# Causal heads in another order, with a bank for their projections and one for sums and values, and compact weights for the folds

## The reference

```python
x = x + tanh(g_xattn[0]) * L0_xattn(layernorm(x), ctx)      # 16 heads of 64, no mask
x = x + tanh(g_ffn[0]) * L0_ffn(layernorm(x))               # ternary weights, 8-bit activations
x = x + tanh(g_xattn[1]) * L1_xattn(layernorm(x), ctx)
x = x + tanh(g_ffn[1]) * L1_ffn(layernorm(x))               # one gated expert, gelu

def L1_xattn(xx, ee):
    x = ln(xx); x = x + mha_a1(x, x, causal)    # 16 heads of 32 over 512 tokens
    x = ln(x);  return x + mha_a2(x, ee)        # 16 heads of 32 over 77 tokens

def mha(x, y, causal):
    q, k, v = ln(x) @ wq, ln(y) @ wk, ln(y) @ wv
    a = softmax(q @ k.T / sqrt(D))              # the softmax runs over all 512 keys
    if causal: a = a * (key > query)            # the mask comes after it
    x = x + concat(a @ v) @ li1 + li1_b
    return x + gelu(ln(x) @ li2 + li2_b) @ li3 + li3_b
```

## Time and profile before

| | us |
|---|---|
| median of 3 runs | 419.72 (417.35 to 419.81) |
| the profiled execution | 419.06 |
| its span | 417.2 |
| PE, PEld busy | 346.0 (83%), 237.8 (57%) |
| DVE, ACT, POOL busy | 307.4 (74%), 279.2 (67%), 114.6 (27%) |

### The profile page before, as it was taken

The page is one execution under the profiler, slowest core; times in us unless marked ns, Lnnn a source line. Parts: engine busy times, 40 slices in busy tenths (PEclk is TensorE's granted clock), DMA queues, the critical chain, the costliest instruction groups (busy, mean ns, idle before and its releaser), DMA issues.

```text
span 417.2 us, 6788 instructions
## 1 busy us (share of the span) xinstructions
PE 346.0 (83%) x2038; PEld 237.8 (57%) x2038; DVE 307.4 (74%) x718; ACT 279.2 (67%) x965; POOL 114.6 (27%) x215
## 2 busy tenths in 40 slices
PE   4978999636377779999798898988997899977796
PEld 4756888513233445555554545567775678853656
DVE  3656678679874798999999899865776787845515
ACT  4465998758134887898888888825626889854061
POOL 5312875200110222232232223323001354420000
PEclk9999999986558999999999999989999899998999
DMA  7920000000003836832951690000000000000001
GB/s 215 348 110 2 2 2 2 0 1 2 0 20 94 198 94 147 183 76 68 206 132 37 149 207 15 2 2 1 2 2 0 0 3 0 2 0 2 1 0 52
DMA packets 8861, 24.75 MB, mean 59 GB/s; under 512 B 2668, under 2 KB 2745, under 8 KB 8569
## 3 DMA queue, kind: packets, MB, share of 16 engines
q1 hardware_dynamic: 8824, 24.32, 23.0%
HBM read 7.00 MB, written 0.52 MB: 18 GB/s over the span
## 4 chain that ended last, share of the span: by engine, by line
PE 41%; DVE 15%; ACT 8%; issue 7%; SPq 2%; POOL 1%; DMA 0%; DVEq 0%; ACTq 0%
PE ps L400 8%; PE ps L540 5%; PE ps L524 5%; DVE nm L1532 4%; PE ps L670 4%; PE ps L618 3%; ACT pring L1145 3%; PE ps L633 3%; PE ps L493 3%; PE ps L473 3%; PE ps L704 2%; PE ps L441 2%; ACT arena L1022 2%; PE ps L686 2%; DVE xn L1216 2%
## 5 line engine op out<-in xcount | busy, mean ns | idle before, releaser
L1145 ACT ACTIVATE pring<-ps,nm 128x512 f32<-128x512 f32 x128 | 87.0, 687 | 12.7 <-DVE nm L1532 9.7
L1022 ACT ACTIVATE arena<-ps,nmx 128x77 f32<-128x77 f32 x256 | 79.1, 343 | 13.9 <-DVE nmx L1294 13.9
L1532 DVE TENSOR_REDUCE nm<-ps 128x2 f32<-128x1024 f32 x64 | 78.0, 1219 | 5.6 <-PE ps L633 5.4
L909 POOL TENSOR_SCALAR_AFFINE_SELECT pring<-pring 128x128 f32<-128x128 f32 x128 | 38.6, 301 | 109.2 <-ACT pring L1145 109.2
L633 PE MATMUL ps<-Ks,Qs 128*128 128x512 f32 x128 | 53.0, 467 | 7.9 <-ACT pring L1145 3.8
L400 PEld LDWEIGHTS ps<-ident,pring 128*128 128x128 f32 x352 | 39.4, 140 | 33.3 <-issue 18.0
L400 PE MATMUL ps<-ident,pring 128*128 128x128 f32 x352 | 52.2, 277 | 7.3 <-ACT xn L1112 3.2
L1022 ACT ACTIVATION_READ_ACCUMULATOR arena<-ps,nmx 128x1 f32 x256 | 57.1, 223 | 0.0
L881 POOL TENSOR_TENSOR arena<-arena,rden 128x616 f32<-128x616 f32 x32 | 39.2, 1226 | 54.1 <-DVE rden L1299 54.1
L872 POOL TENSOR_TENSOR rstd<-var,minus_half 128x4 f32<-128x4 f32 x18 | 18.2, 1011 | 105.7 <-DVE var L1209 105.7
L493 PE MATMUL ps<-arena 128*128 128x128 f32 x320 | 42.4, 280 | 5.8 <-DVE arena L1306 5.8
(11 more groups left out here) (145 smaller groups left out, 540.7 us busy)
## 6 DMA issues: line engine op xcount, KB each, us to landing
Qs<-qh SPq DMA_DIRECT2D x24, 128.0 KB, 2.4
Qs<-ql SPq DMA_DIRECT2D x24, 128.0 KB, 2.4
Ks<-xo SPq DMA_DIRECT2D x24, 128.0 KB, 2.4
Ks<-xb SPq DMA_DIRECT2D x24, 128.0 KB, 2.4
wa_sb<-in_wa SPq DMA_DIRECT2D x1, 1536.0 KB, 14.9
early<-in_w SPq DMA_DIRECT2D x2, 512.0 KB, 7.7
wa_sb<-in_wa SPq DMA_DIRECT2D x1, 1024.0 KB, 17.3
Qs<-hid SPq DMA_DIRECT2D x16, 64.0 KB, 2.0
```

The lines of the kernel that those rows point to most:

```text
L909: pool.affine_select(out=blk, in_=blk, compare_op=ALU.is_gt, fill=0.0, base=0, pattern=[[1, P]], channel_multiplier=-1).then_inc(masked, 1)
L1022: ins = act.activation(Pc[:, i % PC_SLOTS, h * HS:h * HS + M], bank(where[key])[:, h % 4 * HS:h % 4 * HS + M], ACT.Exp, bias=nmx[:, i % 4, ...
L1145: release(act.activation(pring[:, n % 2, i, :], bank(f"S{i}"), ACT.Exp, bias=nm1[:, n % 8, i:i + 1], accum_out=den1[:, n % 8, i:i + 1]), ( ...
L1532: dve.tensor_reduce(nm1[:, n % 8, 2 * u:2 * u + 2], pair(u), AX.X, ALU.max, negate=True).then_inc(nm1_ready, 1)
```

## The change

1. **Order of the heads.** `head(n)` now goes batch by batch: eight heads (a table t of two projection pairs) make two groups of four in the count of `values`, and consecutive heads alternate between two row groups e of projections. Stacks and halves hold the two e of one batch instead of two batches. There are three sets of halves in turn (the third one in a spare part of the arena).
2. **What precedes the loop.** Only batch 0 is normalised and projected (four projections, m = 0 to 3) ahead of it. Batch 1's statistics, normalisation and transposes come at heads 0, 2 and 4, and its layer norm ln1 on DVE stands behind the four low halves and two value copies. Projections come at heads 0 and 2 (two each, in B and A), then one at the end of each even head from 6 to 20, in bank B. Value tiles 4 to 7 come at heads 8, 12, 16 and 20, in A.
3. **Sums and values.** The transposed sums go to bank A at the end of heads n with n mod 4 = 1 (the last ones to B), `values(k, (3, 2))` follow at the end of those with n mod 4 = 2, `values(k, (1, 0))` and four more matmuls of 128 columns in the middle of n mod 4 = 3, where `normalise` is too.
4. **Pieces.** Piece 2 has three blocks and not the unused one. PT has another layout. ACT copies piece 2 of every other head, DVE that of the rest. The broadcast rdx moves from DVE to POOL, behind the masks of the head with n mod 4 = 3.
5. **Folds.** The context operand is compact, without zeros and their memsets, copied once per group of projections. Each head's 64 or 32 rows are multiplied alone, 154 columns, with the next head's rows in another bank right behind it. Copies take 462 (l0) or 308 (a2) columns; of the second l0 fold ACT copies two of six.

```diff
-        PIECES = [[(0, 0), (0, 1), (0, 2), (0, 3)], [(1, 1), (1, 2), (1, 3)], [(2, 2), (3, 2), (2, 3), (3, 3)]]
-        LATE_VALUES = [0, 1, 6, 8]
+        PIECES = [[(0, 0), (0, 1), (0, 2), (0, 3)], [(1, 1), (1, 2), (1, 3)], [(2, 2), (2, 3), (3, 3)]]
         NHB = NB * H
 
+        def head(n):
+
+            t, j, e = n // (2 * HG), n % (2 * HG) // 2, n % 2
+            return t // 2, j, e, HG * (2 * (t % 2) + e) + j
...
+        def next_projections(n):
+
+            if n in (0, 2):
+                return [(4 + n, "B"), (5 + n, "A")]
+            return [(5 + n // 2, "B")] if n % 2 == 0 and 6 <= n <= 20 else []
+
...
+        def pt_copier(n, piece):
+
+            if piece == 0:
+                return pt_act, n + n // 2 + 1
+            if piece == 1:
+                return pt_dve, n + (n + 1) // 2 + 1
...
-                    claim(pe, res, ("fold", site, kv, n),
-                          read_by=fold_copies[site, kv, n][1:])
-                    filled(pe.matmul(bank(res)[:, 0:H // FOLD[site]["n"] * len(bs) * M], wx(k),
-                                     src[:, k, :, bs[0]:bs[-1] + 1, :], start=True, stop=True),
-                           ("fold", site, kv, n))
+                f, src = FOLD[site], heads_kv[site][kv]
+                wx = f["wo" if kv else "wq"]
+                banks = ("T0", "T1", "A", "B") if site == "l0" else ("T0", "T1", "A")
+                uses = fold_uses(site)
+                for n in range(0, len(uses), 2):
+
+                    ks = uses[n][0]
+                    pe.wait_ge(proj_ready, proj_before(site, kv) + ks[-1] // 3 + 1)
+                    both = range(n, n + 2)
+                    for m in both:
+                        claim(pe, banks[m % len(banks)], ("fold", site, kv, m), read_by=fold_copies[site, kv, m][1:])
+                    for i, k in enumerate(ks):
+                        for m in both:
+                            d_of = slice(uses[m][1] * f["d"], (uses[m][1] + 1) * f["d"])
+                            ins = pe.matmul(bank(banks[m % len(banks)])[:, i * NB * M:(i + 1) * NB * M],
+                                            wx(k)[d_of, :], src[d_of, k, :], start=True, stop=True)
+                            if i == len(ks) - 1:
+                                filled(ins, ("fold", site, kv, m))
...
-                    pe.wait_ge(pt_act, n1)
-                    pe.wait_ge(pt_dve, 2 * n1)
+                    pe.wait_ge(pt_act, n1 + n1 // 2)
+                    pe.wait_ge(pt_dve, n1 + n1 // 2)
                     claim(pe, "A", ("o1", k), read_by=(OT_ready, k + 1), filled_by=(pv1_done, k + 1))
+
+                def weighted(jb, h, c0, c1, at_block, start, stop):
+                    n = HG * k + h
+                    d0 = head(n)[3] * D1
+                    return pe.matmul(bank("A")[h * D1:(h + 1) * D1, c0 * P:c1 * P], V[:, b * NT + jb, d0:d0 + D1],
...
                 if 0 in key_blocks:
+
+                    for h in range(HG):
+                        m = weighted(NT - 1, h, NT - 1, NT, 14, True, True)
                     filled(m, ("o1", k))
 
             def sums_transposes(k):
                 pe.wait_ge(rdx_ready, k + 1)
-                res = next_T()
+                res = "A" if k < NGRP - 1 else "B"
                 claim(pe, res, ("rt", k), read_by=(RT_ready, k + 1))
                 transposes(("rt", k), res, lambda t: rdx[:, t, :, :].rearrange("p h d -> p (h d)"), NT)
...
-            for n in range(NHB + 3):
-                k = (n - 1) // HG - 1
+            for n in range(NHB + 2):
+                k = n // HG - 1
                 if n < NHB:
                     scores(n, 0)
-                if n in LATE_VALUES:
-                    project_values(NT + LATE_VALUES.index(n), "B" if n else "A")
-                if next_projection(n):
-                    project(next_projection(n))
+                    scores(n, 1)
                 if 1 <= n <= NHB:
                     p_transposes(n - 1, 0)
                     p_transposes(n - 1, 1)
+                if n >= HG and n < NHB and n % HG == 3:
+                    values(k, (1, 0))
                 if n < NHB:
-                    scores(n, 1)
-                if n >= HG and n % HG == 1:
-                    values(k, (3,))
-                if n >= HG and n % HG == 2:
-                    values(k, (1, 0))
+                    scores(n, 2)
+                    scores(n, 3)
                 if 1 <= n <= NHB:
                     p_transposes(n - 1, 2)
+                if n >= HG and n % HG == 1:
+                    sums_transposes(k)
+                if n >= HG and n % HG == 2:
+                    values(k, (3, 2))
+                if n == NHB + 1:
+                    values(k, (3, 2, 1, 0))
+                for m, res in next_projections(n):
+                    project(m, res)
+                if n == 4:
+                    ln_transposes("a1", 1)
+                if value_tile(n):
+                    project_values(value_tile(n), "A")
                 if n == NHB:
                     li1(0)
-                if n >= HG and n % HG == 1:
-                    values(k, (2,))
-                if n >= HG and n % HG == 2:
-                    sums_transposes(k)
 
             pe.wait_ge(ctxT_ready, 2)
...
+                if n % HG == HG - 1:
+
+                    k = n // HG
+                    pool.wait_ge(rd1_ready, k + 1)
+                    if k:
+                        pool.wait_ge(RT_ready, k)
+                    pool.tensor_copy(rdx[:, :, :, :], rd1[:, :, :].rearrange("p h t -> p t h").unsqueeze(3)
+                                     .to_broadcast([P, NT, HG, D1])).then_inc(rdx_ready, 1)
...
             def sums_across(k):
 
+                if k:
+                    act.wait_ge(OT_ready, k)
                 res = await_bank(act, ("rt", k))
                 release(act.activation(RT[:, :], bank(res), ACT.Copy), ("rt", k))
...
                         act.wait_ge(nm1_ready, 2 * n + u + 1)
@@ -1145,10 +1182,17 @@
                             release(act.activation(pring[:, n % 2, i, :], bank(f"S{i}"), ACT.Exp,
                                                    bias=nm1[:, n % 8, i:i + 1], accum_out=den1[:, n % 8, i:i + 1]),
                                     ("s1", n, i))
-                if n > HG and n % HG == 2:
-                    sums_across(n // HG - 1)
-                if n in LATE_VALUES[::2]:
-                    copy_values(NT + LATE_VALUES.index(n))
+                    if u == 0 and 1 <= n <= NHB and n % 2 == 0:
+                        pt_copy(n - 1, 2)
+                    if u == 0:
+                        for m, _ in next_projections(n - 1):
+                            high_half(m)
+                    if u == 0 and n >= HG and n % HG == 2:
+                        sums_across(n // HG - 1)
+                if n == NHB + 1:
+                    sums_across(NGRP - 1)
+                if n == 5:
+                    a1_evac(1)
 
             project_context("a2", 1)
             ln_evac("a1f", 0, ("a1_ln3_g", "a1_ln3_b"))
...
             f0_out(1)
             ln_norm("a1", 0, x1)
+            for m in range(4):
+                low_half(m)
+            copy_values(1)
+            copy_values(3)
             ln_stats("ln1", 1, r)
             ln_norm("ln1", 1, r, ("ln1_g", "ln1_b"), x1)
-            low_half(0)
-            low_half(1)
-            ln_stats("a1", 1, x1)
-            copy_values(1)
-            copy_values(3)
-            ln_norm("a1", 1, x1)
...
             def inverse_sums(k):
 
                 dve.wait_ge(exp1_done, NT * HG * (k + 1))
+                if k:
+                    dve.wait_ge(rdx_ready, k)
                 j0 = HG * k % 8
-                did(dve.reciprocal(rd1[:, :, :], den1[:, j0:j0 + HG, :]))
-                settle()
-                dve.tensor_copy(rdx[:, :, :, :], rd1[:, :, :].rearrange("p h t -> p t h").unsqueeze(3)
-                                .to_broadcast([P, NT, HG, D1])).then_inc(rdx_ready, 1)
...
-                    if u == 1 and next_projection(n):
-                        low_half(next_projection(n))
-                    if 1 <= n <= NHB:
+                    if 1 <= n <= NHB and (u == 0 or n % 2):
                         pt_copy(n - 1, 1 + u)
-                if n in LATE_VALUES[1::2]:
-                    copy_values(NT + LATE_VALUES.index(n))
-                if n >= 1 and n % HG == 0 and n <= NHB:
-                    inverse_sums(n // HG - 1)
+                    if u == 0 and HG <= n <= NHB and n % HG == 0:
+                        inverse_sums(n // HG - 1)
+                    if u == 0 and value_tile(n - 1) and value_tile(n - 1) % 2:
+                        copy_values(value_tile(n - 1))
+                for m, _ in next_projections(n - 1):
+                    low_half(m)
+                if n == 0:
+                    ln_stats("a1", 1, x1)
```

307 lines of the change are left out of this document (145 added, 162 removed).

## The result

The changed kernel takes 435.97 us (median of 4 runs, 435.5 to 437.21), the kernel before 418.54 (4 runs, 414.9 to 419.81): ratio 1.0447, 95% interval 1.0379 to 1.0514. The forecast was 427.8, with a range up to 434.5. The profiled execution took 435.5 (before 419.06), its span is 433.8 (before 417.2), its mean granted clock 0.929 (before 0.947). DVE's busy time fell from 307.4 to 285.9 us and its idle time ahead of the row maxima rose from 5.6 to 34.4.

The account below looks back on a forecast made before the run. DVE was taken to pace the head loop. Loop +11.1, tail +0.4, a2 folds -0.9 and layer 0 -2.5 sum to +8.1 on 419.06: 427.2 profiled, 427.8 against the median; range 412.5 to 434.5.

Parts of the forecast that it names:

- The wait for the sums: Head loop: first value matmul waits for ACT's copy of the sums in bank A; 1.93 us lost in each of seven groups.
- Rival 1: Head loop: the wait for the sums costs nothing and the lighter DVE decides; 413.3 us, chance 0.15.
- rival 2: Head loop: part of the wait is absorbed, half of the 13.5 us; about 421, chance 0.17.
- Groups with projections: Head loop, four groups of four heads: 20.0 us each against 17.5 before, +2.5 per group.
- batch 1's work: Start of the loop, nm(0) to nm(6): it lies in these heads, with steps of 3.75, 4.4, 3.9, 4.4, 3.55 and 4.55.
- the slots of PT: Transposed-probability buffer: six slots free one head later; hidden in a plain group, 0.26 us with a projection.
- The folds of a2: Folds in the a2 stage: DVE's eight copies decide, 3.7 us per fold against 4.2; -0.9 for both.
- Rival 3: Head loop: PE's clock falls in each of seven groups, about 1 us longer each; 435, chance 0.15 together with Rival 4.
- Rival 4: Folds: row groups do not overlap, costing 0.7 each more; 432, chance 0.15 together with Rival 3.
- Start and layer 0: Layer 0 folds and copies -2.5 us; start of the head loop up to nm(6) -3.4 us.
- The tail: Behind the last exponential: last sums in bank B wait for DVE to read the first output product; +0.4 us.
- DVE as the pace of the loop: Head loop before the change: DVE paces it; the change saves DVE 1.46 us per group in copies and 0.35 more.

Follow-up runs that it names:

- e2: Changed kernel with ScalarE's copy of the sums moved ahead of the two first exponentials of its head; 420.39 us in one run.
- f2: Changed kernel with sums copied first, a2 folds over four banks, and a group's last values ahead of the transposes; 413.36 us, 0.9896 of the kernel before.
- e3: Changed kernel with a2 folds issued one use after the other, each claiming its own bank; 433.61 us in one run, stage F 27.86.
- e4: Changed kernel with every second copy of the a2 folds on ScalarE; 436.04 us, stage F 33.39.
- f3: Changed kernel with sums copied first, a2 folds over four banks and issued use by use; 412.78 us in one run, stage F 27.93.
- g1: f2 with the a2 folds issued use by use as in e3; 415.06 us, 0.9913 of the kernel before.
- g4: g1 with piece 2 of every head copied by VectorE; 412.54 us, 0.9890 of the kernel before.

## Why the prediction was wrong, point by point

**The wait for the sums** was found, placed and sized rightly. PE stood 1.69 to 2.06 (forecast 1.9), and it costs 1.9 in each group with projections (forecast 1.93) and 1.7 in the last one without (e2). A group without projections takes 17.52 (forecast 17.5), with steps of 5.99, 4.63, 3.35 and 3.55 for 6.0, 4.5, 3.7 and 3.3. e2 undoes it and gives 15.8. Rival 1 (the wait costs nothing) is excluded, and so is rival 2 (half of it absorbed): none of it was.

**Groups with projections** take 21.50, 20.60, 20.15 and 20.22, not 20.0 each. More than half of these 2.4 us is not the group's: the step at nm(6) is 8.18, those at nm(10), nm(14) and nm(18) are 6.83 or 6.84, and ACT's two copies of batch 1's transposes stand ahead of its probability copy and exponentials:

```profile
155.63 0.78 ACT L993 ACTIVATE xnT<-ps,cols_sb 128x512 f32<-128x512 f32 x1
...
156.29 0.78 ACT L993 ACTIVATE ynT<-ps,cols_sb 128x512 f32<-128x512 f32 x1
```

The forecast had batch 1's work in the heads before, with 4.55 for the step at nm(5), which took 3.54. That the slots of PT hold ACT's copy was priced at 0.26, and f2 recovers 0.26. What makes up the rest, 0.15 to 0.6 per group, stays open; no run has more slots.

**The folds of a2** are the step that failed. "In the a2 stage the copies then decide, eight of 0.51 each on DVE", so 3.7 per fold, took DVE's busy time for its pace. The changed code claims banks in pairs from three, and each pair waits for a copy of the last: 1.42 each, 5.1 per fold. The claims in pairs stand in the diff; only their chain was not followed. The stage costs +5.4 for -0.9: 6.3 of the 8.5 us missed, some 2.8 of it in the folds themselves and 3.2 in the two products behind them, which run partly at the low clock. e3, which changes the claims alone, gives back 5.5.

**The clock.** Rival 3 was right in kind. It was priced for the loop alone, and there it struck one group of seven in the profiled execution (2.7 us) and up to three in others (e3, e4). It was not considered behind the folds, where it costs 3.2; together that is 5.9, the largest part of what the forecast lacks. The prediction compared busy shares over 20 us (16.0 of 20.0, near 21.98 of 27.16) and took them for safe; the runs show falls behind 7.18 of 9.16 and 5.92 of 7.95, and behind about 6.2 of 7.7 one way in f3 and the other in g1, so such shares did not tell the two cases apart.

**Rival 4** is excluded: row groups overlap (2.6 times). The fixed 0.02 per matmul in its price of 4.9 stands in no row. The Trainium skill (TensorE: Matmul & The Clock Gate, Measured speedup vs the span model) has 3.07 for four row tiles, and the trace agrees in kind. The Trainium skill (TensorEngine Tiling (Array Packing), PSUM Bottleneck) names the copies as what may bound next, which the trace bears out in that DVE's copies release every pair; it was the round trip and not the copying rate that counted (e4).

**Start and layer 0** came as forecast: -2.9 and -4.3 for -2.5 and -3.4. **The tail** gained 1.5 where a loss of 0.4 was forecast. The marks show that 0.1 of it lies ahead of the first output product and 1.4 between the two products (274.64 to 284.83, now 287.17 to 295.94). The first product alone accounts for that:

```profile
274.64 5.37 PE L704 MATMUL ps<-wa_sb,hid 128*128 128x128 f32 x32
...
287.17 3.74 PE L741 MATMUL ps<-wa_sb,hid 128*128 128x128 f32 x32
```

The upper line is of the kernel before, with a clock of 0.62 there, the lower one of the changed kernel at 1.00. As far as the runs show this is luck and nothing that the change does: e3 and e4 took 5.12 and 5.03 for the same product. The other terms were 11.7 us too small together, and the start and the tail made up for 3.2 of it. **DVE as the pace of the loop** was wrong as a reading of the kernel after the change: DVE lost 1.8 us of work per group, and g4 gave about half of that back (0.9) at no cost.
